# Eight images in one straight program: a convolution, Mamba and experts kernel without the barrier between images

## The reference, cut to what matters

```python
for each of 8 images x (56 x 56 tokens, 64 channels):
    # layer 0: 32 narrow paths (1x1 to 4 channels, 3x3, 1x1 back to 64), batch norms and relus, summed, plus x, relu
    x = relu(x + sum(path_p(x) for p in range(32)))
    # layer 1: layer norm, a Mamba block forward and one backward over the 3136 tokens
    hs  = associative_scan(combine, (exp(dt * A), dt * B * u))      # 128 channels x 16 states, both directions
    x  = x + out_proj(forward) + out_proj(backward)
    # experts: layer norm, router, the top 2 of 8 experts (64 -> 256 -> 64, gelu), weighted sum, plus x
```

## Time and profile before

| | |
|---|---|
| time, median of 3 runs | 5216.6 us (5200.36 to 5223.23) |
| the profiled execution: its time | 5213.57 us |
| its span, first to last instruction | 5211.8 us |
| first scan starts, last scan starts | 274.4 us, 5074.3 us |
| busy: PE, DVE, POOL, ACT | 84%, 77%, 75%, 64% of the span |
| mean granted TensorE clock | 0.937 of full speed |

### The profile page before, as it was taken

The page is one execution under the profiler, slowest core; times in us unless marked ns, Lnnn a source line. Parts: engine busy times, 40 slices in busy tenths (PEclk is TensorE's granted clock), DMA queues, the critical chain, the costliest instruction groups (busy, mean ns, idle before and its releaser), DMA issues. The chain is left out here.

```text
span 5211.8 us, 70837 instructions
## 1 busy us (share of the span) xinstructions
PE 4357.3 (84%) x21206; PEld 1771.7 (34%) x21206; DVE 4025.3 (77%) x6073; ACT 3334.8 (64%) x5405; POOL 3922.9 (75%) x4937
## 2 busy tenths in 40 slices
PE   3577788888888888888889888789888888888887
PEld 1233333333333333333333333333333333332332
DVE  2278887888877887888878888788878788788771
ACT  1255566767666766676767676667666676676665
POOL 1277787888877887888878888788878888788772
PEclk9588999999999998999999999899999999999997
DMA  2365564555555654555545555455555555554420
GB/s 66 72 148 141 134 140 114 138 131 136 125 118 118 140 132 106 135 136 129 133 113 134 131 133 127 109 137 136 130 116 131 128 135 127 115 117 106 98 62 5
DMA packets 255558, 623.33 MB, mean 120 GB/s; under 512 B 105268, under 2 KB 170676, under 8 KB 255028
## 3 DMA queue, kind: packets, MB, share of 16 engines
q1 hardware_dynamic: 255156, 618.60, 51.5%
HBM read 540.85 MB, written 77.65 MB: 119 GB/s over the span
## 5 line engine op out<-in xcount | busy, mean ns | idle before, releaser
L1193 POOL TENSOR_TENSOR hc<-hs,cb 128x448 f32<-128x448 f32 x1792 | 2030.5, 1136 | 751.6 <-DVE hs L1030 726.9
L1030 DVE TENSOR_TENSOR_SCAN hs<-dtb,state,ps 128x448 f32<-128x448 f32 x1792 | 2047.4, 1143 | 105.8 <-issue 1.8
L1020 DVE TENSOR_TENSOR ps<-ps,bb 128x448 f32<-128x448 f32 x1792 | 1098.7, 613 | 443.9 <-PE ps L687 437.9
L865 ACT ACTIVATE dtb<-dtb,decay 128x448 f32<-128x448 f32 x1792 | 1086.2, 657 | 198.4 <-DMA dtb<-dt_scratch 193.5
L687 PE MATMUL ps<-dux,pick 128*128 128x448 bf16 x3584 | 1049.1, 374 | 164.6 <-DVE hs L1030 102.5
L907 ACT ACTIVATE hg<-ps,be 128x448 f32<-128x448 f32 x896 | 520.1, 631 | 430.5 <-PE ps L751 429.0
L687 PE MATMUL ps<-duz,pick 128*128 128x448 bf16 x1792 | 649.2, 362 | 0.0
L751 PE MATMUL ps<-xn,we 64*128 64x448 f32 x1792 | 583.3, 621 | 53.5 <-ACT hg L907 53.0
L687 PEld LDWEIGHTS ps<-dux,pick 128*128 128x128 bf16 x3584 | 264.6, 99 | 865.4 <-issue 527.8
L734 PE MATMUL ps<-h,w 96*128 96x448 bf16 x896 | 313.0, 385 | 212.5 <-ACT rz L896 86.3
L699 PE MATMUL ps<-hc,gather 128*32 128x448 f32 x3584 | 454.2, 580 | 8.7 <-POOL hc L1193 8.4
(11 more groups left out here) (175 smaller groups left out, 6277.2 us busy)
## 6 DMA issues: line engine op xcount, KB each, us to landing
dtb<-dt_scratch SPq DMA_DIRECT2D x448, 896.0 KB, 6.6
slab<-h_scratch SPq DMA_DIRECT2D x168, 290.0 KB, 8.1
dt_scratch<-sp SPq DMA_DIRECT2D x112, 224.0 KB, 2.0
h_scratch<-h2p SPq DMA_DIRECT2D x168, 112.0 KB
h<-h_scratch SPq DMA_DIRECT2D x56, 336.0 KB, 4.1
h_scratch<-h1s SPq DMA_DIRECT2D x56, 232.0 KB, 3.9
xw<-xn_scratch SPq DMA_DIRECT2D x112, 112.8 KB, 2.6
xw<-xn_scratch SPq DMA_DIRECT2D x112, 112.5 KB, 2.7
```

Of the source, the lines that this page charges most:

```text
L865: A.activation(a, a, ACT.Exp, scale=decay[k % 2][:, i:i + 1]).then_inc(a_ok, 1)
L1020: V.tensor_tensor(bank, bank, bb[:, k % 2, :], ALU.mult).then_inc(bu_ok, 1)
L1030: V.tensor_tensor_scan(rev(hs[:, n % RH, :], d), rev(dtb[i // 4][:, i % 4, :], d), rev(bank, d), state[:, d, i:i + 1], ALU.mult, ALU.add). ...
L1193: P_.tensor_tensor(hc[:, n % 8, :], hs[:, n % RH, :], cb[:, k % 2, :], ALU.mult).then_inc(hc_ok, 1)
```

## The change

The calls of `emit`, the loop, the clears and the barriers between images go. There is one block in which every engine walks the slots from the first convolution (slot -226) to the last output, with one set of semaphores whose counts run through all eight images. One clear and one barrier are left at the end, and those of the setup.

What follows from that:

- the memset of `state` goes; the first step of each direction scans with `zeros`, a tile of 128 x 1 zeros, as its initial value;
- `gather_y`, `gate`, `out_proj` and `add_out` of the last step of an image, which stood at the end of a call, move to slots 3 and 6 of the next image, where the other steps have theirs; `spread_dt(k, 3)` of an image's step 0 moves from the start of the call to slot 1, as in the other steps;
- `decays_to` runs ahead over the boundary too;
- waits that a barrier had made needless are there now: `tokens_in` waits for `o_rd` at each chunk, `fetch_res` for the `fold` of the image two back, `soft_in`, `copy_bb`, `spread_dt` and others for their counts across the boundary;
- since `add_out` of the last step (chunk 0) comes only at slot 6 of the next image, the experts take chunk 6 ahead of chunk 0: `E_ORD["mid"]` swaps the two; for that `x_in` moves from 6 to 10 slots behind the chunk's start, and `paths` stays at 14.

The core of it, without the lines that only lose indentation:

```diff
-E_ORD = {"mid": (3, 4, 0, 6, 1, 5, 2), "last": (3, 4, 2, 5, 1, 6, 0)}
+E_ORD = {"mid": (3, 4, 6, 0, 1, 5, 2), "last": (3, 4, 2, 5, 1, 6, 0)}
...
-SLOTS = G + 2
+LAST = NB * STEPS
+END = NB * G
...
-        "split2": -5, "put2": -4, "arrange": -4, "z": 6, "x_in": 6, "paths": 14, ...
+        "split2": -5, "put2": -4, "arrange": -4, "z": 6, "x_in": 10, "paths": 14, ...
...
+        SLOTS = range(min(slots.values()) - 2, max(slots.values()) + 4)
...
                     def fetch_res(it):
                         c = A_ORD[it[1]]
-                        if it[0] - 2 in e_imgs:
-                            old = (it[0] - 2, E_ORD[e_imgs[it[0] - 2][0]].index(c))
-                            after(m_dve, by_dve("fold", old))
+                    if it[0] >= 2:
+                        after(m_dve, by_dve("fold", (it[0] - 2, E_ORD["mid"].index(c))))
...
-                    if run:
-                        spread_dt(0, 3)
-                    for n in range(SLOTS):
+                for n in SLOTS:
...
-                            if i == 1 and 1 <= k and run:
+                    if i == 1 and 0 <= k < LAST:
                                 spread_dt(k, 3)
...
-                            if i == 3 and k:
+                    if i == 3 and 1 <= k <= LAST:
                                 gather_y(4 * k - 1)
-                            if i == 6 and k:
+                    if i == 6 and 1 <= k <= LAST:
                                 out_proj(k - 1)
...
-                        while run and decays[0] <= min(n, G - 1):
+                    while decays[0] <= min(n, END - 1):
                             dA(decays[0])
...
-                                             state[:, d, i:i + 1], ALU.mult, ALU.add).then_inc(h_ok, 1)
+                                         state[:, d, i:i + 1] if k % STEPS >= 2 else zeros[:, :], ...
...
-                        if it[0] == 0:
-                            dve.wait_ge(o_rd, last_step(c) + 1)
+                    dve.wait_ge(o_rd, STEPS * it[0] + last_step(c) + 1)
...
-                    if run:
-                        V.memset(state[:, :, :], 0.0).then_inc(st0, 1)
-                        dve.wait_ge(st0, 1)
-                        weigh_b(0)
...
-        emit(1, False, {1: ("first", 0)}, {})
-        emit(0, True, {0: ("first", 0), 1: ("mid", 1)}, {0: ("mid", 0)})
-        with nc.Fori(1, NB - 1, 2) as img:
-            emit(1, True, {0: ("mid", img), 1: ("mid", img + 1)}, {-1: ("mid", img - 1), 0: ("mid", img)})
-            emit(0, True, {0: ("mid", img + 1), 1: ("mid", img + 2)}, {-1: ("mid", img), 0: ("mid", img + 1)})
-        emit(1, True, {0: ("mid", NB - 1)}, {-1: ("mid", NB - 2), 0: ("last", NB - 1)})
-        emit(0, False, {}, {-1: ("last", NB - 1)})
```

More of the change, by code:

```diff
@@ L260, in _ @@
                 pool.memset(zero, 0.0).then_inc(s_pool, 1)
+                pool.memset(zeros[:, :], 0.0).then_inc(s_pool, 1)
                 pool.memset(gather[:, :], 0.0).then_inc(s_pool, 1)
@@ L1340, in build, with a_class @@
[L1340 to L1346 removed]
+        def a_class(r):
+            return "mid" if r else "first"
@@ new lines, in build, with now, upto, upto_side @@
+        SLOTS = range(min(slots.values()) - 2, max(slots.values()) + 4)
+        of_stage, at_slot = {}, {}
+        for (side_, what, of), n in slots.items():
+            of_stage.setdefault((side_, what), []).append(of)
+            at_slot.setdefault((side_, what, n), []).append(of)
+        def now(side_, what, n):
+            return at_slot.get((side_, what, n), [])
+        def upto(side_, what, of):
+            return sum(x <= of for x in of_stage[side_, what])
+        def upto_side(side_, what, of):
+            return sum(x <= of and side(x) == side(of) for x in of_stage[side_, what])
@@ new lines, in earlier, with total @@
+        def earlier(side_, what, n):
+            return sum(slots[side_, what, of] < n for of in of_stage[side_, what])
+        def total(side_, what):
+            return len(of_stage[side_, what])
+        RING = []
+        for what in ("x_T", "paths_in", "second", "norm_T"):
+            RING += [(slots["A", what, of], 1, what, of, "act") for of in of_stage["A", what]]
+        RING += [(slots["A", "third", of], 1, "third", of, "act" if of[1] in ACT_J else "dve")
+                 for of in of_stage["A", "third"]]
@@ new lines, in build, with misc_made, misc_act @@
+        for what in ("tokens_T", "logits", "fold"):
+            MISC += [(slots["E", what, of], what, of) for of in of_stage["E", what]]
+        MISC = sorted(MISC, key=lambda job: job[0])
+        misc_at = {job[1:3]: q for q, job in enumerate(MISC)}
+        misc_in = {}
+        for q, job in enumerate(MISC):
+            misc_in.setdefault(job[0], []).append(q)
+        def misc_made(what, of):
+            return misc_at[what, of] + 1 if (what, of) in misc_at else 0
+        def misc_act(q):
+            return sum(job[1] not in ("fold", "logits") for job in MISC[0:q])
@@ L1349, in _layouts @@
+        for s in loop_sems:
+            nc.gpsimd.sem_clear(s)
+        nc.all_engine_barrier()
 def _layouts(np, I):
```

1563 lines of the change are left out of this document (757 added, 806 removed).

## The result

The changed kernel takes 5048.28 us (median of 4 runs, 5044.54 to 5058.17) against 5218.66 us of the kernel before measured beside it: a ratio of 0.9683, 95% interval 0.9656 to 0.971. The profiled execution took 5048.39 us with a span of 5046.6 us, 165.2 us less than the span before.

The account below looks back on a forecast made before the run. No engine was at its limit, so waits at image borders and slow running behind them bound the kernel. Gains 78.3 + 40.9 + 8.2 + 9 = 136.4 us gave 5077.2 us, 5080 against the median; range 5045 to 5125.

Parts of the forecast that it names:

- The gaps: Seven borders, last scan of an image to first of the next: each becomes an ordinary 3.68 us interval, gain 78.3 us.
- that rival: Borders: a new wait drains the pipeline anyway, without the clears; 50 us gain left, 5166 us; chance 0.05.
- W0: First 32-slot stretch of images 1 to 7: 88.8 us each falls to 83.0, gain 40.9 us.
- The clock share: Part of W0's extra time from TensorE's lower clock: about 5 us of PE work for each W0.
- The two reasons for a slow W0: Behind a border: ACT's seven exponentials in a row (4.02 us), and TensorE's granted clock falling in the gap.
- Prologue to image 0: Start of the run: first scan at 266.2 us in place of 274.39, gain 8.2 us.
- Image 7 to the tail: End of the run: the tail's first matmul follows the last experts at once, gain 9 us, bounds 5 and 14.
- the tight `x_in`: Residual load before `paths_out`: 2.0 us early to 3 us late, costed at nothing; slower-by-it rival had chance 0.03.
- the new waits: Waits across the border: a queue entry each, met long before, costed at nothing.
- the length of the program: Straight program in place of the loop: instruction traffic hardly changes; even doubled under 1% of the DMA engines.
- Only the gaps go: Rival: W0 keeps its 88.8 us; gain 95.5 us, 5121 us, up to 5138; chance 0.15.
- More comes back: Rival: W1 gains too, freed of W0's late work, with larger W0 and tail gains; 173 us, 5043 us; chance 0.12.

Follow-up runs that it names:

- b_burst: b_clear with ACT's exponentials held back to each border, so that each image starts with seven in a row: 5205.85 us, ratio 0.9969.
- b_sync: The changed kernel with a bare all-engine barrier put back at the nine borders, without clears: 5134.7 us, ratio 0.9825.
- the drain: b_burst with the last step's gather, gate, projection and addition of each image put back ahead of the barrier: 5245.0 us, ratio 1.0051.
- b_clear: b_sync with 65 clears of a spare semaphore by GpSimd ahead of each barrier: 5169.19 us, ratio 0.9886.
- warm: The kernel before with 20 needless matmuls on PE at the end of each image's call, ahead of clears and barrier: 5238.94 us, ratio 1.0031.
- the b_ runs: Four kernels putting a border's parts back into the changed kernel, each on top of the one before: 5134.7, 5169.19, 5205.85 and 5245.0 us.
- rows_mix: mix with the third chunk's input rows brought in ten slots later: 5066.13 us, ratio 0.9694.
- rows_ahead4: The changed kernel with exponentials 4 slots ahead in place of 6 and the third chunk's input rows ten slots later: 4965.09 us, ratio 0.9528.
- ahead4: The changed kernel with ACT's exponentials 4 slots ahead of the scan in place of 6: 4990.46 us, ratio 0.9561.
- mix: The changed kernel with exponentials 4 slots ahead only in slots 7 to 11 of each 32, 6 elsewhere: 5118.03 us, ratio 0.979.
- sync4: b_sync with exponentials 4 slots ahead in place of 6: 5056.33 us, ratio 0.9677.

## Why the prediction was right, step by step

- **The gaps: exact.** 78.4 us against 78.3. The interval of 3.68 us from inside an image held at the border (3.67), since the tables do repeat there. So no new wait drained the pipeline at the border, and that rival (5166 us) fell.
- **W0: right in kind, the gain too small.** 54.8 us against 40.9. The mis-sized term is the 83.0 us for a W0, which I set above a "lower bound" of 82.1 us. It measured 81.0 us, below that bound, because both numbers were means over stretches that partly ran at the lower clock: of the six W6 27 us before and 7 us after, of the eighteen W2 to W4 51 us before. W0 after the change hardly does: its time at the lower clock fell from 103 to 14 us over seven, and 89 x 0.54 = 48 us are most of the 54.8. The clock share that I put at 5 us for each W0 was thus nearer 7. The Trainium skill's rule ("TensorE: Matmul & The Clock Gate", section "Why this matters for your kernels"), that an idle gap between bursts puts the array back to its lower clock, gave 35 us in place of 40.9. The trace agrees with its direction: the gaps ran at 0.66 to 0.72, and all seven W0 began at the lower level.
- **The two reasons for a slow W0: one shown, one open.** b_burst shows the burst: ACT's seven exponentials ahead of all else make W0 4.1 us longer, with 39 us more at the lower clock over seven W0. That is half of the 7.8 us. The other half came with a bare barrier: W0 goes from 81.0 to 85.2 us in b_sync, to 84.3 with the clears, 88.4 with the burst and 89.1 with the drain (88.8 before). A long slow gap alone is thus not enough, since b_clear's gaps at 0.71 to 0.82 left W0 no longer than b_sync's at 1.00. How much of the rest is the clock carried over from the gap is not shown: warm was to tell, but left PE idle ahead of W0 as before. I had named the burst and the clock, but not the stop itself.
- **Prologue to image 0: 8.2 us forecast, 10.4 measured.** The step itself gave 12.17 - 3.76 = 8.4 us. The other 2.0 us are that the last matmuls of the prologue start at 260.19 in place of 262.22 us; no run shows why.
- **Image 7 to the tail: 9 us forecast, 22.9 measured.** The removed stop gave 11.12 - 1.55 = 9.6 us, as worked out (9.5). The rest, 13.3 us, is the tail at a clock of 0.86 in place of 0.73, with PE busy 82.4 us in place of 96.4. My bound of 14 us named that possibility, but for its first part alone; it was the mis-sized term. The stretch behind the last scan grows with each step of the b_ runs: 117.9 us with a bare barrier, 121.8 with the clears, 127.7 with the burst, 137.6 with the drain. The step of the burst has no exponentials in the tail to explain it; the clock there goes from 0.85 to 0.79. In warm, with needless matmuls in the gap ahead of it, the tail ran at 0.79 and took 10.5 us less; that is one place in one execution.
- **Sum.** 136.4 us forecast against 165.2: W0 13.9, tail 13.9, prologue 2.2, and 1.2 lost elsewhere. The forecast was one of durations at a mixed clock, and both large misses go with less time at the lower clock. That the sum still came within 29 us of the span rests on the gaps, which were exact, and not on W0 and the tail, which were both short by 13.9 us.
- **Costed at nothing, and rightly:** the tight `x_in` (used 14.8 us after its issue, as in the estimate, landed in 4.2 us and not 12.8), the new waits, the swapped tables, the length of the program.
- **The rivals.** "Only the gaps go" fell with W0. "More comes back" gave 5043 us, nearer the time than my forecast, and its terms for W0 (47.2 us) and the tail (14) were nearer too, though still too small. That its sum fits is luck in part, because its own mechanism, W1 freed of late work, did not come: W1 became 1.0 us longer. I had put W1's length down to its extra matmuls. Most of it comes of where the third chunk's rows stand, as rows_mix and rows_ahead4 show: moved ten slots on, with 6 of the 12 extra matmuls, they leave W1 at 84.1 us.

**What stays open.** Why the lower clock comes more often when a barrier is added whose own gap is 1.5 us longer and runs at full clock: half of W0's part of it (27 of 54 us) stands in the first 20 us behind the gap, the rest lies further on. In every profile slot 13 of a stretch has more falls of the clock than any other slot (17 of 45 in ahead4, 34 of 66 after the change, 52 of 78 in mix). It stands behind the place where PE waits for ACT's `rz`. I took ACT's wait for `dtb` as what sets the falls off. The runs do not single it out: it is gone in ahead4 with 222 us at the lower clock, in sync4 with 313 and in mix with 461. PE's wait for `rz`, 3.0 us in place of 1.9, goes with the greater number of falls in slot 13 of mix and rows_mix. Why a wait of 1.9 us is followed by a fall in some stretches and not in others is not shown. Nor is it shown how much of the 0.54 us is the slow matmuls and how much is a stall that made the clock fall.

## What to carry to other kernels

Judge a barrier in a pipelined kernel by what runs behind it, not by its gap: here bare barriers lengthened the gaps by 10.5 us in all and the run by 86. When terms are taken from rows, note the granted clock of each row and compare only stretches at the same clock, since a mean over mixed stretches hides what a removed stall gives back. After a structural change, try the look-ahead and the hand-set order again: they gave 83 us more here. When a look-ahead changes between two depths, look at the slot of the change: in mix the exponentials caught up there in a row and PE waited for ACT, and the run was 70 us slower. And before a run with added work is read as a test, look whether the wait that the work was to fill is gone; in warm it was not.

## What the hardware showed that I had not expected

- Needless matmuls in a gap raised the clock there (0.69 to 0.83 in the mean), but 5.2 to 8.9 us of idle time were left behind them, and seven W0 gained nothing: 621.2 against 621.9 us. The tail behind such a gap took 115.9 us in place of 126.4.
- PE's wait for one eviction, 3.0 us in place of 1.9, was followed by a spell of the lower clock in 19 and 21 of 24 stretches (mix, rows_mix) in place of 5 to 13.
- The time inside the images of nine kernels that differ only at their borders, in the loop, in a table or in a slot of `arrange` spreads from 4639 to 4738 us, and follows their time at the lower clock (309 to 457 us) with a correlation of 0.99.
- 65 clears of a semaphore ahead of a barrier cost 5.2 us for each border, though a clear is recorded with 44 ns, 2.9 us for 65.
